# Target one-hots made once, stored in DRAM and loaded again in a later pass of a graph kernel

## The reference, cut to what matters

```python
# layer 1: one message per edge, summed by target
h = jnp.concatenate([x[row], edge_attr], axis=1)
h = jnp.maximum(h @ W1a + b1a, 0.0) @ W1b + b1b
ssum = jax.ops.segment_sum(h, col, num_segments=x.shape[0])
...
# layer 2: the message depends on source and on the edge's type
for r in range(num_relations):
    mask = (edge_type == r)[:, None]
    msg = jnp.where(mask, x_src @ weight[r], 0.0)
    out = out + jax.ops.segment_sum(msg, dst, num_segments=num_nodes)
```

## Time and profile before

| | |
|---|---|
| median of 3 runs | 4458.94 us (4453.23 to 4469.04) |
| profiled execution, first to last instruction | 4502.7 us |
| edge pass, in the profile | 2222 to 2685 us |
| relation pass, in the profile | 2883 to 3567 us |
| near pass / far pass, in the profile | 3680 to 3975 us / 4100 to 4450 us |
| PE / DVE / ACT / POOL busy over the span | 70% / 72% / 32% / 31% |

### The profile page before, as it was taken

How to read it: one execution, slowest core, us unless ns; L and a number is a source line. 1 busy time by engine, 2 the same in 40 slices (tenths; PEclk the granted TensorE clock), 3 DMA queues, 4 the chain that set the end, 5 groups by cost and what they waited for, 6 DMA issues and landing times. The chain is left out here.

```text
span 4502.7 us, 84639 instructions
## 1 busy us (share of the span) xinstructions
PE 3132.8 (70%) x29061; PEld 2437.5 (54%) x29061; DVE 3224.2 (72%) x7791; ACT 1435.4 (32%) x2737; POOL 1405.7 (31%) x1198
## 2 busy tenths in 40 slices
PE   0087777777238348158499985588888769959995
PEld 0054444444102112112499984287888769959995
DVE  7766666665489699699577763377767579967886
ACT  0034444444025125035399981233333200000000
POOL 0055555555264454554000000266666300000000
PEclk9978888888569679579699996599999879979997
DMA  8845555545458358267377740111111024413331
GB/s 323 322 129 143 153 144 148 157 131 149 147 172 264 114 166 263 88 200 246 106 221 221 222 148 12 56 24 23 24 23 24 14 67 111 109 28 102 88 91 47
DMA packets 413507, 587.19 MB, mean 130 GB/s; under 512 B 76420, under 2 KB 301787, under 8 KB 412709
## 3 DMA queue, kind: packets, MB, share of 16 engines
q1 hardware_dynamic: 366005, 447.98, 34.2%
q0 software_dynamic: 37728, 66.91, 5.5%
q10 hardware_dynamic: 9360, 66.90, 3.7%
HBM read 340.05 MB, written 234.93 MB: 128 GB/s over the span
## 5 line engine op out<-in xcount | busy, mean ns | idle before, releaser
L846 POOL DMA_INDIRECT slots<-bc_rec,idx x496 | 484.6, 977 | 410.4 <-ACT bc_rec L807 294.4
L1284 POOL DMA_INDIRECT rp_rows<-rel_rows,slot_rel x390 | 412.1, 1057 | 431.7 <-POOLq L118 182.3
L1106 PE MATMUL psum<-a_probs,z 128*65 128x512 f32 (+1 forms) x1050 | 445.7, 557 | 145.0 <-DVE a_probs L1039 145.0
L1320 DVE TENSOR_SCALAR rp_hot_src<-rp_key_rows,lane 128x384 bf16<-128x384 f16 x1560 | 383.5, 317 | 202.0 <-issue 88.5
L1534 PE MATMUL psum<-rel_pieces,rp_hot_src 128*128 128x192 bf16 x4680 | 452.1, 249 | 94.3 <-issue 75.8
L1074 ACT ACTIVATE a_tops<-a_tops,a_s_low 128x1024 f32<-128x1024 f32 (+2 forms) x300 | 284.1, 947 | 569.6 <-DVE a_tops L1030 569.1
L1534 PEld LDWEIGHTS psum<-rel_pieces,rp_hot_src 128*128 128x128 bf16 x4680 | 390.4, 99 | 128.8 <-issue 107.0
L483 POOL DMA_INDIRECT slots<-h,idx x192 | 327.6, 1706 | 352.3 <-DMA h<-recs 304.1
L1106 PEld LDWEIGHTS psum<-a_probs,z 128*65 128x65 f32 x1050 | 121.8, 137 | 469.4 <-DVE a_probs L1039 301.5
L703 DVE TENSOR_SCALAR bc_first_t<-bc_ramp,bc_key_t 128x128 f16<-128x128 f16 x500 | 136.5, 273 | 307.8 <-PE psum L729 172.7
L1030 DVE SCALAR_TENSOR_TENSOR a_tops<-table,a_s_rest,big 128x1024 f32<-128x1024 f32 (+2 forms) x300 | 309.3, 1031 | 32.8 <-DMA big<-shift_rows 32.8
(11 more groups left out here) (438 smaller groups left out, 6855.1 us busy)
## 6 DMA issues: line engine op xcount, KB each, us to landing
a_counts<-edge_counts SPq DMA_DIRECT2D x150, 512.0 KB
slots<-big ACTq DMA_DIRECT2D x65, 1005.0 KB
ep_rec<-slots SPq DMA_DIRECT2D x65, 1005.0 KB, 6.2
edge_counts<-bc_counts SPq DMA_DIRECT2D x12, 3125.0 KB
hot_rows<-ep_hot_src SPq DMA_DIRECT2D x325, 96.0 KB, 4.5
sp_hot_src<-hot_rows SPq DMA_DIRECT2D x325, 96.0 KB, 2.0
sq_hot_src<-hot_rows SPq DMA_DIRECT2D x325, 96.0 KB, 2.0
a_counts<-edge_counts SPq DMA_DIRECT2D x75, 282.5 KB
```

Of the source, the lines that this page charges most:

```text
L846: pool.indirect_dma_start(k.slots, bass.IndirectOffsetOnAxis(k.idx[:, first + t:first + t + 1], 0), rec[:, j, t, :], None).then_inc(scatte ...
L1106: last = nc.tensor.matmul(sums[:, a:b], k.z[:, s, 0:D + 1], probs[:, a:b], start=s == 0, stop=True, skip_group_check=True)
L1284: pool.indirect_dma_start(rows[:, n % ROW_SLOTS, s, 0:width], None, table, bass.IndirectOffsetOnAxis(k.slot_rel[:, at:at + 1], 0))\
L1320: last = v.tensor_scalar(hot_src[:, n % HOT_SLOTS, rel, :], key_rows[:, n % 2, :], k.lane[:, rel:rel + 1], None, ALU.is_equal)
```

## The change

The edge pass still makes all 325 target one-hots on DVE. After each, POOL copies it into a third ring of four buffers (`keep` in float32, or `keep16` in bf16 for the chunks that the relation pass looks up, padded from 252 to 256 columns), and SP stores the copy in DRAM right behind the store of that chunk's source one-hot. The relation pass makes none on DVE: SP loads them, into `DST_SLOTS` = 8 buffers of each kind, and `add_up` waits for the load. DVE's `hot_target(c)` of the edge pass gets one more wait (that POOL has copied chunk c - 4), and SP's queue of the relation pass gets 325 loads, with `place` between them.

```diff
+        self.dst_rows = nc.dram_tensor("dst_rows", (NCHUNK, P, SLOTS * BIN_ROWS), FP32, kind="Internal").ap()
+        self.dst_rows16 = nc.dram_tensor("dst_rows16", (NCHUNK, P, DST_COLS), BF16, kind="Internal").ap()
...
+    ROW_SLOTS, DST_SLOTS, MSG_SLOTS, SUM_SLOTS, KEEP = 8, 8 if relations else 4, 4, 3, 4
...
                             sp.dma_start(k.hot_rows[n, :, :], hot_src[:, n % HOT_SLOTS, :]).then_inc(hot_io[n % HOT_SLOTS], 16)
+                        store_target(c)
+
+                def store_target(c):
+                    sp.wait_ge(kept, c + 1)
+                    if by_lookup(c):
+                        sp.dma_start(k.dst_rows16[c, :, :], keep16[:, c % KEEP, :]).then_inc(dst_out[c % KEEP], 16)
+                    else:
+                        sp.dma_start(k.dst_rows[c, :, :], keep[:, c % KEEP, :]).then_inc(dst_out[c % KEEP], 16)
+
+                def load_target(c):
+                    if c >= DST_SLOTS:
+                        sp.wait_ge(added, c - DST_SLOTS + 1)
+                    y = c % DST_SLOTS
+                    if looks_up(c):
+                        sp.dma_start(hot_dst16[:, y, :], k.dst_rows16[c, :, :]).then_inc(dst_in[y], 16)
+                    else:
+                        sp.dma_start(hot_dst[:, y, :, :].rearrange("p s r -> p (s r)"), k.dst_rows[c, :, :])\
+                            .then_inc(dst_in[y], 16)
...
+                    for y in range(KEEP):
+                        sp.wait_ge(dst_out[y], 16 * len(range(y, NCHUNK, KEEP)))
+                elif relations:
+                    for c in range(NCHUNK):
+                        done = c - DST_SLOTS - 3
+                        if done >= NT and done % NT == 0:
+                            place(done // NT - 1)
+                            placed_to = done // NT
+                        load_target(c)
...
+                def keep_target(c):
+                    y = c % KEEP
+                    pool.wait_ge(dst_made, c + 1)
+                    if c >= KEEP:
+                        pool.wait_ge(dst_out[y], 16 * (c // KEEP))
+                    to = keep16[:, y, 0:SLOTS * BIN_ROWS] if by_lookup(c) else keep[:, y, :]
+                    nc.gpsimd.tensor_copy(to, hot_dst[:, c % DST_SLOTS, :, :].rearrange("p s r -> p (s r)")).then_inc(kept, 1)
+
+                if edges:
+                    nc.gpsimd.memset(keep16[:, :, SLOTS * BIN_ROWS:DST_COLS], 0.0)
+                    for c in range(NCHUNK):
+                        keep_target(c)
...
+                        if edges:
+                            dve.wait_ge(kept, c - DST_SLOTS + 1)
...
-                    hot_target(c)
+                    if not relations:
+                        hot_target(c)
...
-                    pe.wait_ge(dst_made, c + 1)
+                    if relations:
+                        pe.wait_ge(dst_in[c % DST_SLOTS], 16 * (c // DST_SLOTS + 1))
+                    else:
+                        pe.wait_ge(dst_made, c + 1)
```

More of the change, by code:

```diff
@@ L143 @@
 BIN_ROWS = max(end - first for first, end in map(bin_rows, range(BINS)))
+DST_COLS = 256
+assert SLOTS * BIN_ROWS <= DST_COLS
 def bin_parts(b):
@@ L1158, in edge_pass @@
     SPELL_AHEAD, LOOK_AHEAD = 6, 3
-    ROW_SLOTS, DST_SLOTS, MSG_SLOTS, SUM_SLOTS = 8, 4, 4, 3
     edges, relations = kind == "edges", kind == "relations"
+    ROW_SLOTS, DST_SLOTS, MSG_SLOTS, SUM_SLOTS, KEEP = 8, 8 if relations else 4, 4, 3, 4
     HOT_SLOTS = 2 if relations else 8
@@ L1180, in edge_pass @@
         hot_io = [sem(f"hot_io{y}") for y in range(HOT_SLOTS)]
+        kept = sem("kept")
+        dst_out = [sem(f"dst_out{y}") for y in range(KEEP if edges else 0)]
+        dst_in = [sem(f"dst_in{y}") for y in range(DST_SLOTS if relations else 0)]
         found = FIELD if edges else width
@@ L1187, in edge_pass @@
             square = sb("square", [P, 2, SLOTS * P])
+            keep = sb("keep", [P, KEEP, SLOTS * BIN_ROWS])
+            keep16 = sb("keep16", [P, KEEP, DST_COLS], BF16)
         if relations:
@@ L1191, in edge_pass @@
             hot_src = sb("hot_src", [P, 2, RELS, SLOTS * P], BF16)
-            hot_dst16 = sb("hot_dst16", [P, DST_SLOTS, SLOTS, BIN_ROWS], BF16)
+            hot_dst16 = sb("hot_dst16", [P, DST_SLOTS, DST_COLS], BF16)
             msg = sb("msg", [P, MSG_SLOTS, SLOTS, 3 * D], BF16)
@@ L1259, in _ @@
                         sp.wait_ge(hot_io[y], 16 * len(range(y, len(LOOKUPS), HOT_SLOTS)))
-                elif not relations:
+                    for y in range(KEEP):
[8 more added lines that the diff above has]
+                else:
                     for n in range(len(LOOKUPS)):
@@ L1326, in hot_target @@
                         dve.wait_ge(added, c - DST_SLOTS + 1)
-                    to = hot_dst16 if relations and looks_up(c) else hot_dst
+                        if edges:
+                            dve.wait_ge(kept, c - DST_SLOTS + 1)
                     shape = [P, SLOTS, BIN_ROWS]
-                    v.tensor_tensor(to[:, c % DST_SLOTS, :, :], k.bin_lane[:, :].unsqueeze(1).broadcast_to(shape),
+                    v.tensor_tensor(hot_dst[:, c % DST_SLOTS, :, :], k.bin_lane[:, :].unsqueeze(1).broadcast_to(shape),
                                     slots(k.slot_dst, c).unsqueeze(2).broadcast_to(shape), ALU.is_equal)\
@@ L1561, in add_up @@
                             got = msg[:, LOOKUP_NO[c] % MSG_SLOTS, s, :]
[L1562 to L1565, removed]
+                            one = hot_dst16[:, y, s * BIN_ROWS:(s + 1) * BIN_ROWS]
+                            nc.tensor.matmul(to, one, got[:, 0:2 * D], start=first, stop=True, skip_group_check=True)
+                            last = nc.tensor.matmul(to[:, 0:D], one, got[:, 2 * D:3 * D], start=False, stop=True,
+                                                    skip_group_check=True)
                         else:
```

## The result

The change makes the kernel slower: 4551.69 us (4547.53 to 4554.95, 4 runs) against 4458.95 (4453.23 to 4469.04, 4 runs), +93 us. The ratio of the runs is given as 1.0216, 95% interval 1.0202 to 1.0231 (the two medians by themselves give 1.0208). The prediction was 4468, with a range to 4500. The profiled execution of the changed kernel spans 4553.2 us and so stands for its plain runs, while the one of before was 44 us longer than its own; the two profiles differ by only 50.5 us, and stages are compared instead of spans.

A forecast was written before the change was run, and what follows sets the result against it. It took PE and ACT to bound the edge pass, and waits the relation pass, with a PE floor of 530 us. -3 (relation) and +12 (edge) gave +9: 4468 us from 4458.9, range 4438 to 4500.

The forecast's parts named there:

- Relation half: Relation pass: removing 325 target one-hots (122.7 us of DVE) gains only 3 us, bounds 0 and -27; loads cost 0.
- rival B: Relation pass: a target one-hot is in the ring that sets the pace; -27 us, 4432 in all, chance 0.17.
- within 5 us of 684: Sign that the forecast is right: the relation pass stays this close to its 684 us.
- POOL's copies: Edge pass: 325 copies on idle POOL, 0.29 to 0.58 us each, 94 to 190 us in all, off the path.
- Ring of four stores: Edge pass: waiting for a copy four chunks back costs 0 unless a store lands late; 5.4 against 5.7 us.
- SP's issue: Edge pass: one load and ten stores take SP 6.05 us of a group's 7.12, leaving 1.07 to spare.
- Rival C: Edge pass: SP or the ring of four stores becomes the bound; +36 less 3, 4492 in all, chance 0.18.
- A: The forecast itself: SP late behind each `place` in the edge pass; 4468 us, own range 4450 to 4482, chance 0.45.
- PE hit only behind a `place`: Edge pass: later record loads cost PE 1.2 us, 11 times, 13 us less about 1: +12 us.
- DMA share 67 to 87%: Edge pass: 29.6 MB on top of 95.5 MB raises the DMA engines' share; records land an estimated 1 us later.
- D: Edge pass: POOL's copy and DVE's one-hot exclude each other; 4465 to 4517 us, taken as 4485, chance 0.05.
- E: Whole kernel: all is hidden and little is gained; 4456 to 4462 us, chance 0.15.

The follow-up runs named there:

- e3_rel_none: Kernel before, without target one-hots or their loads in the relation pass (sums left out): 4155.69 us against 4171.51, ratio 0.9965.
- e1_edge_half: Kernel before plus the edge pass's copies and stores only; the relation pass makes its own one-hots: 4257.98 us against 4171.51, ratio 1.0198.
- e2_keep7: Changed kernel with seven instead of four buffers in POOL's ring of copies: 4196.15 us against 4171.51 for the kernel before, ratio 1.0054.
- e10_keep5: Changed kernel with five instead of four buffers in POOL's ring of copies: 4487.55 us against 4459.21 for the kernel before, ratio 1.0067.
- e7_pool_queue: Changed kernel with seven buffers and the stores issued by POOL instead of SP: 4525.09 us against 4486.06 for the kernel before, ratio 1.0083.
- e8_by_groups: Changed kernel, two target stores per five-chunk group behind the next record load, three group buffers: 4476.33 us against 4459.21 for the kernel before, ratio 1.0039.
- e6_small_stores: Only the edge pass's copies and stores, seven buffers, 32 columns per store: 4495.99 us against 4486.06 for the kernel before, ratio 1.0023.

## Why the prediction was wrong

**What bounded the kernel: right.** PE and ACT were full in the edge pass, and what held PE up cost time at once: its new idle time (55 us) and the slower clock after its stops (29) are the 84. The relation pass's floor of 530 us was met by e3_rel_none (531.0).

**Relation half, -3 us (bounds 0 and -27): right that most of the 122.7 us is off the path, the size too small.** Taking them away altogether brings 9.9 us on one chip and 15.8 on another (7.6 in the pass itself), inside the bounds; rival B's -27 did not come. The relation pass was 664.8, outside the "within 5 us of 684", but a kernel that makes its one-hots there shows 659 to 682 in profiles, so that test could not decide. DVE's busy time fell to 378.8, not to 359: I subtracted 122.7 from 481.4, but the groups of the earlier trace rows overlap (380.4 + 122.7 = 503.1 in 481.4 busy), and only the part not overlapped comes off. The loads cost nothing in that pass on the fast chip (531.7 with them, 531.0 without). In the totals the gain is not seen: the whole changes are at +93 and +94 us and the edge half alone at +87, each against the kernel before on its own chip and with up to 15 us of uncertainty.

**POOL's copies, 0.29 to 0.58 us off the path: right** (397 ns, ratio 1.0002).

**Ring of four stores, "5.4 against 5.7 us for four chunks": the step that failed.** The sum had this ring at nothing. Its 4.5 us was a median over the source stores of the kernel before, and the store that matters is not a median one: the first target store of each group is issued behind 1005 KB of records. It lands in 5.3 us by the median, the fifth in 2.1 (e1_edge_half); 5.5 us passed from its issue to POOL's copy at 2407.39, and 7.3 in the next turn. And the comparison was with the chunks' own pace, as if a late store only held POOL. I wrote "SP behind it" and did not follow it: the fifth store of a group is followed in SP's queue by the next record load. A ring of four under a group of five closes a circle: record load, first target store, its landing, fifth copy, fifth store, next record load. It takes 7.66 and 9.16 us where shown, and 8.47 on average by the pass's length. The slack of DVE cannot absorb it, because it comes again in every group. Five buffers remove 62 us of the 84, seven 52 (full stores) and 55 (small ones).

**SP's issue, 6.05 us a group: too small.** Behind one another, load and ten stores took 6.9 us by the median in e2_keep7 and 6.4 in e10_keep5; the 6.05 came from one group with five stores of one kind. Rival C's threshold of 0.58 us a DMA was passed with 0.62, and its 500 us for the pass is close to the 497.1 that seven buffers leave. In the changed kernel itself this is hidden under the ring: SP still waits 182.5 us there (the rows of its waits and `place`'s 5.9; between issues its queue stands still for 110), where I expected "well under 100" for A.

**PE hit only behind a `place`, "That happens 11 times": the second step that failed.** It gave the +12. I had not looked at how early a record load lands: 0.7 us before it is needed. With the ring open DVE still waits for records in 56 and 59 of 65 groups (five and seven buffers), 122 and 140 us in all, and the pass is 22 to 32 us longer. With the issues taken off SP, or with fewer of them, it is still longer by 17 and 15 us (e7_pool_queue and e8_by_groups), and there the records land in 7.9 and 8.3 us. Late source stores have a part in it too (18 of PE's 30 us of stops in e2_keep7 are put down to ACT's source one-hot); how the loss divides between the two is not shown.

**DMA share 67 to 87%: right once the ring is open** (87.1 and 86.0%). The records' landing, guessed 1 us later, was 6.0 us in the changed kernel, 6.8 with five buffers, and 8.3 in e8_by_groups.

**The rivals.** C came nearest: it named this ring, but priced only SP's issues (+36), and gave it 0.18; the loss was 84 us in the pass. Neither of its two signs, PE gaps in every group and SP without waits, came as stated: DVE waits for records in 59 of 65 groups, but PE stops for over 0.1 us in 33 (15 before), and SP waits. They are signs of the issue-bound case, which the runs with an open ring are near to, and not of the ring. A, B, D and E fall.

No version of the whole change that was tried beats the kernel before. Taking the one-hots out of the relation pass brought at most 16 us, and storing the 29.6 MB in the edge pass, where PE and ACT are busy for 98% of the time, cost at least 15 (481.0 against 466).

## What to carry to other kernels

When stores of a ring share a queue with the loads that feed the pass, count the ring in *groups between two loads*, not in chunks: a ring shorter than the group couples each load to the landing of a store behind the previous load, and then the latency is the pace. Price such a landing by the store issued right behind the largest transfer, and the issue of DMAs by a stretch where as many stand back to back as will after the change. Read from the trace before how long each load has landed when it is first needed: that, and not the idle time of the queue, is what the change may use up. Before moving work out of a pass, take it out altogether once: if that brings 10 to 16 us of 123, the work was under cover there.

## What the runs showed of the hardware that was not expected

**The same kernel takes 4171.5 us on one chip, and 4459 and 4486 on two others, and the difference lies in some stages.** The edge pass is the same (465.2 and 466.6), the relation pass is not (538.6 against 682.4). Of the 333 us between the two profiles 144 are in the relation pass and 190 ahead of the edge pass. Around 3000 us, inside that pass in both, the first profile of before and the one on the fast chip show, columns as in the earlier trace rows:

```profile
3000.00:3100.00 100.00, 84.41 (x1052) 78.25 (x1049) 70.79 (x279) 33.68 (x89) 59.03 (x58) 0.98 0.13 23
```

```profile
3000.00:3100.00 100.00, 96.21 (x1299) 95.64 (x1297) 88.73 (x344) 41.07 (x107) 78.36 (x72) 1.00 0.15 28
```

On the one chip PE stops for 15.6 of 100 us while POOL gathers, put down to "issue", and gets through 1052 matmuls; on the other it gets through 1299. All four profiles of the fast chip have 531 to 540 us in this pass, all ten of the others 648 to 690. So the 150 us "while the gathers run" that the prediction took from the earlier trace rows come with the chip that ran and not with the kernel alone: on the fast chip PE is busy for 494.8 of 500 us with gathers going on. By what mechanism gathers hold up PE on one chip and not on another stays open. Each chip was used in one stretch of time only, so a chip cannot be told from the conditions of its hour. For a reader of profiles: a gap called "issue" beside gathers, on one chip, may not be there on the next.

**A store of 8 KB lands only 1.1 us sooner than one of 126 KB.** The medians are 3.7 us in e6_small_stores and 4.8 in e2_keep7, both with seven buffers. The place behind the record load counts for more: in e6_small_stores the first target store of a group (8 KB) needs 5.0 us by the median, the fifth, also 8 KB, 2.5.

**A copy on POOL stretches when it meets a one-hot of DVE.** It takes 399 ns alone and 676 where the two overlap for 0.4 us or more, in the same pass of the changed kernel.
